# Cross-attention and dequantised linear layer on one core: five Python loops per program turned into loops of the engines

## The reference

```python
q = (layernorm(x) @ wq)   # 32 heads of 128
k = ctx @ wk              # 8 heads, each used by 4 query heads
v = ctx @ wv
q, k = apply_rope(q, pos), apply_rope(k, pos)
attn = softmax(q @ k.T / sqrt(128) + mask)
x = x + (attn @ v) @ wo
# second layer: weights from 4 bit planes and a table of 16 levels per output row
w = take_along_axis(lut4, idx_from_bitplanes(qweight, 4), axis=1)
x = x + layernorm(x) @ w.T + bias
```

## Time and profile before

| what | value |
|---|---|
| median of the runs | 2567.6 us |
| the profiled execution, its own time | 2566.0 us |
| its span | 2564.2 us |
| PE busy | 2510.2 us, 98% |
| DVE busy | 1626.7 us, 63% |
| ACT busy | 1147.0 us, 45% |
| POOL busy | 762.2 us, 30% |
| DMA, share of 16 engines | 26.1% |
| TensorE clock granted | 0.997 of full speed |

### The profile page before, as it was taken

One profiled execution on the slowest core, in us unless ns is written; L12 is line 12 of the kernel. 1 busy time (PEld: TensorE's weight loads), 2 busy tenths in 40 slices (PEclk: granted clock), 3 DMA queues, 4 the chain that ended last, 5 costly groups with the idle time before them and its releaser, 6 DMA issues.

```text
span 2564.2 us, 44480 instructions
## 1 busy us (share of the span) xinstructions
PE 2510.2 (98%) x16704; PEld 2309.5 (90%) x16704; DVE 1626.7 (63%) x4004; ACT 1147.0 (45%) x2844; POOL 762.2 (30%) x914
## 2 busy tenths in 40 slices
PE   8999997999999999999999989999999999999999
PEld 7888986899999999999998888999999999999987
DVE  7777778665656665556665766656566565656554
ACT  5333334554545454444543145544444454545420
POOL 0000002243434333333432143434333333434321
PEclk9999999999999999999999999999999999999999
DMA  7433445121221212121215221221212121212041
GB/s 230 143 129 129 152 136 169 42 75 50 70 59 58 63 62 75 42 75 57 72 35 193 82 96 50 70 59 61 64 58 75 42 79 58 67 57 76 26 160 50
DMA packets 198676, 214.48 MB, mean 84 GB/s; under 512 B 13632, under 2 KB 153152, under 8 KB 198464
## 3 DMA queue, kind: packets, MB, share of 16 engines
q1 hardware_dynamic: 198464, 211.65, 26.1%
HBM read 161.28 MB, written 50.33 MB: 83 GB/s over the span
## 4 chain that ended last, share of the span: by engine, by line
PE 88%; DVE 6%; ACT 2%; issue 2%; DMA 1%; POOL 0%; SPq 0%; ACTq 0%; DVEq 0%; POOLq 0%
PE bank L549 27%; PE bank L629 26%; PE bank L678 7%; PE bank L612 7%; PE bank L580 7%; PE bank L509 5%; PE bank L492 4%; PE bank L600 4%; DVE residual L1126 1%; DMA w_scratch<-small_split 1%; PE bank L468 1%; DVE row_numbers L1019 1%; ACT small_split L716 1%; ACT rope_x L712 0%; DVE small_split L1001 0%
## 5 line engine op out<-in xcount | busy, mean ns | idle before, releaser
L549 PE MATMUL bank<-acts_split,weights_split 128*128 128x256 f32 x6144 | 785.1, 284 | 16.2 <-DVE rope_a L984 15.2
L549 PEld LDWEIGHTS bank<-acts_split,weights_split 128*128 128x128 f32 x6144 | 759.8, 193 | 18.4 <-issue 13.2
L629 PE MATMUL bank<-weights_split,small_split 128*128 128x512 f32 x3072 | 767.4, 398 | 0.0
L629 PEld LDWEIGHTS bank<-weights_split,small_split 128*128 128x128 f32 x3072 | 558.2, 188 | 108.3
L880 ACT ACTIVATE probs<-probs,row_numbers 128x256 f32<-128x256 f32 x512 | 256.5, 502 | 601.3 <-DVE row_numbers L1283 601.0
L1443 POOL TENSOR_SCALAR probs<-probs,row_numbers 128x256 f32<-128x256 f32 x512 | 240.1, 482 | 905.1 <-DVE row_numbers L1288 905.1
L1413 POOL TENSOR_TENSOR weights_split<-raw,weights_split 128x1024 fp32r<-128x1024 f32 x124 | 298.6, 2408 | 301.1 <-ACT weights_split L703 301.1
L1405 POOL TENSOR_TENSOR rope_x<-rope_x,sin_t 128x256 f32<-128x256 f32 x256 | 191.1, 746 | 436.6 <-ACT rope_x L712 436.3
L716 ACT ACTIVATE small_split<-rope_a 128x256 fp32r<-128x256 f32 x288 | 120.3, 418 | 298.4 <-DVE rope_a L997 296.4
L984 DVE SCALAR_TENSOR_TENSOR rope_a<-bank,cos_t 128x256 f32<-128x256 f32 x256 | 108.7, 425 | 225.3 <-ACT rope_x L712 225.3
L1277 DVE CUSTOM_DVE_ANT_0 probs<-bank,mask_tile 128x256 f32<-128x256 f32 x512 | 196.2, 421 | 71.4 <-PE bank L580 67.8
(11 more groups left out here) (76 smaller groups left out, 2637.0 us busy)
## 6 DMA issues: line engine op xcount, KB each, us to landing
raw<-in_L_xattn_wq SPq DMA_DIRECT2D x64, 512.0 KB, 4.5
raw<-in_L_xattn_wo SPq DMA_DIRECT2D x64, 512.0 KB, 3.6
k_scratch<-small_split SPq DMA_DIRECT2D x64, 256.0 KB, 2.1
v_scratch<-small_split SPq DMA_DIRECT2D x32, 512.0 KB, 2.9
small_split<-k_scratch SPq DMA_DIRECT2D x64, 256.0 KB, 2.6
mask_tile<-in_mask_BxSxS_ff SPq DMA_DIRECT2D x64, 256.0 KB, 2.7
small_split<-v_scratch SPq DMA_DIRECT2D x64, 256.0 KB, 2.9
weights_split<-w_scratch SPq DMA_DIRECT2D x16, 1024.0 KB, 6.9
```

The costliest lines, as they stand in the source:

```text
L549: last = pe.matmul(q_ps, wq_s[:, h, c, a, :], xT[:, c, m, b * S:(b + 1) * S], start=c == 0 and i == 0, stop=c == C - 1 and i == 2)
L629: last = pe.matmul(out_ps[part][:, :], o_s[:, u % 2, a, t * P:(t + 1) * P], wo_s[:, h, m, n * BANK:(n + 1) * BANK], start=h == 0 and i == ...
```

## The change

In each engine's program the middle turns are no longer unrolled by Python. `for b in range(1, NB - 1)` becomes `with eng.Fori(1, NB - 1) as b` for stage A (SP, PE, ACT, DVE: one body, six turns), and `for g in range(1, HKV - 1)` becomes `with eng.Fori(1, HKV - 1) as g` for the steps (all five engines, six turns in each of the two halves). The loop variable is a register of the engine. Every wait count in a body then is a register, and so is the DRAM address of a DMA. The first and the last turns stay unrolled.

The second part is a new helper, `hold(eng)`, which increments a semaphore `held` that nobody waits for. It stands between the waits and the instruction at some thirty places, also in the turns that stay unrolled. There the waits are now carried by that semaphore instruction and no longer by the instruction behind it.

The core of the diff (each engine has the same two kinds of edit):

```diff
+        held = sem("held")
...
+        def hold(eng):
+
+            eng.sem_inc(held, 1)
...
                 sp.wait_ge(s_mm, n + 1)
+                hold(sp)
                 sp.dma_start(k_s.bitcast(F32).rearrange("p l n -> p (l n)"), k_scr[g, hf * HB + b]).then_inc(k_in, 16)
...
             batch(0, first=True)
-            for b in range(1, NB - 1):
+            with pe.Fori(1, NB - 1) as b:
                 batch(b)
             batch(NB - 1, last=True)
...
                 step(0, range(2, UNITS + LAG), first=True)
-                for g in range(1, HKV - 1):
+                with pe.Fori(1, HKV - 1) as g:
                     step(g, range(LAG, UNITS + LAG))
                 step(HKV - 1, range(LAG, UNITS + LAG), last=True)
...
                 act.wait_ge(rope_mm, n + 1)
+                hold(act)
                 act.activation(ropes[slot][0][0:H2], product[H2:DK], ACT.Copy, scale=scale)
...
                 dve.wait_ge(rope_in, 2 + n + 1)
+                hold(dve)
                 if scale == 1.0:
...
                 dve.wait_ge(stage_hi, count)
+                hold(dve)
                 dve.tensor_tensor(stage[:, BANK:2 * BANK], src[:, :], stage[:, 0:BANK].bitcast(F32),
...
                             pool.wait_ge(inv_ready, n0 + u + 1)
+                            hold(pool)
                             for t in range(TS):
```

More of the change, by code:

```diff
@@ L370, in batch @@
                     sp.wait_ge(dq_step, b * DQ_STEPS + LEAF7)
+                    hold(sp)
                     sp.dma_start(lut_t, lut_v[b + 1]).then_inc(lut_in, 16)
             batch(0, first=True)
-            for b in range(1, NB - 1):
+            with sp.Fori(1, NB - 1) as b:
                 batch(b)
@@ L415, in half @@
                 load_step(0, first=True)
-                for g in range(1, HKV - 1):
+                with sp.Fori(1, HKV - 1) as g:
                     load_step(g)
@@ L475, in turn_weights @@
                 pe.wait_ge(stage_lo, STAGED // 2 + tile * STAGED)
+                hold(pe)
                 for c in range(C):
@@ L830, in _ @@
             batch(0, first=True)
-            for b in range(1, NB - 1):
+            with act.Fori(1, NB - 1) as b:
                 batch(b)
@@ L941, in half @@
                 step(0, range(2, UNITS + LAG), first=True)
-                for g in range(1, HKV - 1):
+                with act.Fori(1, HKV - 1) as g:
                     step(g, range(LAG, UNITS + LAG))
@@ L1239, in _ @@
             batch(0, first=True)
-            for b in range(1, NB - 1):
+            with dve.Fori(1, NB - 1) as b:
                 batch(b)
@@ L1352, in half @@
                 step(0, range(UNITS + LAG), first=True)
-                for g in range(1, HKV - 1):
+                with dve.Fori(1, HKV - 1) as g:
                     step(g, range(LAG, UNITS + LAG))
@@ L1456, in half @@
                 step(0, range(UNITS + LAG))
-                for g in range(1, HKV - 1):
+                with pool.Fori(1, HKV - 1) as g:
                     step(g, range(LAG, UNITS + LAG))
```

10 lines of the change are left out of this document (8 added, 2 removed).

## The result

The changed kernel took 2588.28 us (median of 4 runs, 2587.26 to 2589.49), the kernel before in the same session 2568.21 (4 runs). The ratio is 1.0079, with an interval from 1.0061 to 1.0097: slower by 20 us. The forecast was 2576, inside a range of 2567 to 2602. The profiled execution took 2588.4 us, with a span of 2586.6 and the clock at 0.996 of full speed, against 2564.2 and 0.997 before. Three other executions of this document, one of the kernel before and two of experiments, took 3240 us or more and are left out of every ratio.

What follows compares the result with a forecast made beforehand. PE, busy 98%, was taken to bound the kernel. Stage B branches 5, stage A 1.5 and holds 1.8 make 8.3 us on 2566.0, 2574.3; that execution was 1.6 under the median, so 2576 us, range 2567 to 2602.

Steps and rivals of the forecast that it cites:

- What bounds the kernel: Whole kernel: PE is busy 98% of the span, and the question is whether PE's own sequencer keeps ahead of the array.
- Register and semaphore instructions on PE: Inside the loop bodies on PE: 4.1 register and branch instructions per unit, 0.6 us, hidden by the full queue; cost 0.
- The taken branches of stage B: Ten on PE between steps: each a fetch of 3.0 us minus 2.5 us, 5 us in all, ends 0 and 35.
- the second stop: Rival at stage B's branches: two fetches in a row, 3.5 us × 10, 2604 us; chance 0.12.
- Why it fetches at all: Stage B branches on PE: by the two-page window rule each of 10 misses, body 1769 instructions against 256 in a page.
- the target is still held: Rival: target held or fetch shorter than the cover, so the ten branches cost nothing; 2570 us, chance 0.32.
- The other engines at the seam: DVE, ACT and POOL between steps: DVE's mask 0.9 us late after a 3.0 us fetch, just held by slack; cost 0.
- Stage A and the holds: Stage A's five branches 0.3 us each, 1.5 us; holds 0.1 us at each of 18 waits in the starts, 1.8 us.
- The slack was not eaten: Rival: waits in the sequencers eat the slack of the chain that paces stage B's units; 2583 us, chance 0.09.
- Nothing became faster: Rival: POOL's split starts after DVE's negation has begun, shortening the chain, paying only at the starts; 2563 us, chance 0.04.
- some 130 and more: Sign in PE's instruction queue: this many packets if each branch fetches, far fewer if the loop is held.
- The forecast's own test: Wrong if idle before the scores exceeds 2 us, the cosine enters PE's mid-step waits, or seams show no idle time.

## Why the prediction was right in sign and short by twelve

**What bounds the kernel: right.** PE is at 100.00 between the seams, and the loss is in its own sequencer.

**Register and semaphore instructions on PE, 0: right.** Away from the seams and the starts no step got longer. One register instruction is 32 to 65 ns long, and neighbours start about 0.1 us apart, under the 0.15 taken.

**The taken branches of stage B: this term was mis-sized.** The prediction had "I take 3.0, the nearest row: 0.5 us × 10 = 5 us". The form of the sum held, and so did the cover: 16 matmuls were queued at the branch. At the seam at 1050.9 the small instructions around the branch took 0.36 us, and 3.57 us of matmuls were left, so the cost is the branch less 3.2 (the prediction: less 2.5, since its 0.15 apiece was too much). The branch was 4.33 us on average and not 3.0. The nearest row, an 8 KB table load from issue to landing, was no good measure. The packet itself is not what is long: on average it lasts 1.07 us, just as the prediction worked out from the earlier trace rows, but it starts 1.9 us after the branch, and the branch is over only 1.4 us after it has ended. 4.33 less 3.2 gives 1.1 us, and 1.1 us is what PE stood idle before the scores in either half; the second half's seams cost 1.35, since matmuls that follow each other overlap by 0.16 us, which a stop takes away, and the first one behind it takes 0.1 us longer. The other part is the second stop, which the prediction had as a rival with 0.12: it is real in the half whose head lies near the end of a piece, but added 0.9 us per seam (11.5 less 6.8, by 5) and not 3.0. At the seam shown the second packet started 1.2 us after the branch was over, and 17 matmuls ran meanwhile. Ten seams: 18.3 us for 5 forecast.

**Why it fetches at all** the prediction put down to the length of the body alone. The runs show that the place counts. A turn of 1768 instructions is held with its head at 0 or 16, where it lies in 7 pieces, and fetched anew with its head at 48, near 90, 219 or 236, where it lies in 8. The rival "the target is still held", with 0.32, would have been right, at its 2570 us, had the heads come to lie in the first 25 of 256 places (0 and 16 were run). In either case the body is the same, so this was a chance that the profile of before could not decide, and the sign of the result was in part luck.

The packets show how the room is spent. 146 less 56 is 90, by ten taken branches 9 each. In the changed kernel every later turn of stage B fetches 9 packets: the 8 pieces of the turn and, last, one that starts 13.1 us ahead of the branch in the first half and 4.3 us ahead in the second. By the places, 195 and 66 instructions are left there, 13.2 and 4.5 us at the step's mean pace: it is the piece beyond the end of the turn, asked for when the last piece is entered. After that the head's piece is gone. With the head at place 0 the first turn fetches 7 packets, of which the last is again the one beyond, and the five turns behind it fetch none: seven pieces of the turn and one beyond are held at the same time, and nine are not. A room of 8 pieces fits all thirteen traces. Where the back edge is announced, the piece beyond is not fetched (6 packets in the first turn), so the 8 pieces of the turn stay.

The Trainium skill, page "Runtime: NRT & Kernel Launch", section "Instruction fetch mechanics", has a taken branch fetch whenever its target is outside a two-page window, and beside that gives TensorE's instruction memory as 128 KiB, 2048 instructions. With the window, which the prediction took, the runs disagree: bodies of 612 and 1224 instructions, and one of 1768 in 7 pieces, branched back in 0.2 us. With the 2048 instructions, which are 8 pieces of 256 and which it passed over, they agree. That prefetch runs on sequentially agrees with the second stop and the ninth packet. The same skill's page "Advanced Engine Details and Errata", section "Engine Queue Depths", gives TensorE 64 entries; the runs show half of that, 32 instructions, 16 matmuls with their loads, queued at the branch at every seam.

**The other engines at the seam, 0: right, by another reason.** The prediction gave DVE a fetch of 3.0 us and had it just covered. There was none: DVE's branches last 0.06 us, the others' 0.045.

**Stage A and the holds.** Forecast 1.5 for the loops and 1.8 for the holds. The holds alone measured 2.7 us; all loops with TensorE's heads in place added 0.1 to that (2569.5 against 2569.4), which can't be told from nothing. In the profiles a later batch of stage A takes 47.0 us before, 47.1 with the holds alone and 47.2 with the loops as well, so the loop costs stage A some 0.1 us per branch where 0.3 was put. The 2.7 us of the holds are 0.5 to 5.4 by their interval, so the 1.8 may be right.

**The rivals.** The slack was not eaten: the cosine is not among PE's waits in the middle of a step. (The 2583 us of that rival need the 1.8 of the starts beside the 8 and the 5; these two alone give 2581.) Nothing became faster. That PE's instruction queue still has "some 130 and more" packets if each branch fetches was the right sign to look for: 146. The forecast's own test, wrong if the idle time is over 2 us at the scores, was not met (0.7 to 1.7 us); what the first half's seams cost, with the stop in the query behind it, is over 2.

## What to carry to other kernels

Before a long body is made a loop, count its instructions and ask how many pieces of the instruction stream it covers from where its head will lie. The same loop cost 18 us or nothing by that alone, so a change that only moves code ahead of it can look like a gain or a loss. Fix the head's place or announce the back edge, and read the duration of the taken branches and the count of instruction packets, not the loop's text. And where the price of a fetch is missing, do not take it from a data transfer: here the packet itself was 1.07 us of a branch of 4.33.

## What the runs showed of the hardware

- On TensorE a turn of 1768 instructions that lies in 7 pieces of 256 (heads at 0 and 16) is held; lying in 8 (48, about 57, 90, 98, 184, 219, 225, 236) it is fetched anew at every taken branch, unless the back edge is announced (56 packets against 146). The piece beyond the end is fetched when the last piece is entered, 13.1 us ahead of the branch with 195 instructions left, and takes up room too.
- A taken branch on TensorE takes 0.2 us where the target is held, and 3.7 to 4.9 us where it is not: 1.9 to the start of the packet, 1.07 for it, 1.4 to the next instruction. Then there are instructions for the rest of the piece only, and a second stop of 0.4 to 1.0 us with 37 instructions left, 1.3 with 31, 1.4 to 1.9 with 20.
- An announced back edge has the head fetched from the time when the last piece of the turn is entered. With 11.4 us left the branch took 0.35 us, with 0.9 us left 1.6 to 1.8, also for a body of 14 pieces that is not held.
- At 3 of the 10 seams with the head at 236 the granted clock fell to the lower level behind the two stops for some microseconds (0.79 over 8 us at the first), which cost some 2 us each; at the other seven, with the same two stops, it did not.
